# Filler writes spread over sixteen pairs, dummies of TensorE moved, and the last loads split over two queues

## The chip, the core and the metric

The kernel runs on one core of a Trainium2 chip. The metric is the device time of one execution in microseconds (us). The kernel before took 531.76 us, the median of three runs (530.24, 531.76, 532.05). A core has five engines that run side by side, each with its own instruction queue and in order: TensorE (PE) for matrix products, VectorE (DVE), ScalarE (ACT), GpSimd (POOL) and SyncE (SP), which here only issues transfers. They wait for each other through semaphores.

## What is computed

The reference, cut to what matters. `x` is 16 sequences of 512 tokens with 128 features.

```python
def wkv_layer(x):                       # first layer, added to x twice: inside and outside
    xn = layernorm(x, g1, b1)
    r, w, k, v = sigmoid(xn @ Wr.T), -exp(xn @ Ww.T), xn @ Wk.T, xn @ Wv.T
    e = exp(w + k)                      # a scan over the 512 tokens of a sequence:
    # num = decay * num + e * v ; den = decay * den + e ; wkv = num / (den + 1e-8)
    x = x + (r * wkv) @ Wo.T
    xn = layernorm(x, g2, b2)
    return x + sigmoid(xn @ Wrec.T) * (square(relu(xn @ Wkey.T)) @ Wval.T)

def moe_layer(h):                       # second layer: 16 experts, one for each token
    score, expert = top1(h @ router_w.T)
    s = sigmoid(score)
    gate, up = split((h * s) @ gate_up[expert])
    routed = (up * silu(gate)) @ down[expert]
    shared = (silu(h @ shared_gate.T) * (h @ shared_up.T)) @ shared_down.T
    return shared + routed

x = x + wkv_layer(layernorm(x))
out = x + moe_layer(layernorm(x))
```

## The kernel before, in words

**Tile stage.** The 8192 tokens are 16 tiles of 512, one sequence each. `one_round(n)` is written once for each engine; in round n the engine does step 0 of tile n, step 1 of tile n-1 and so on, in an order written out by hand, 23 rounds in all. For a tile: `T1` transposes the normed input `xn1tok`, `Ww`, `Wk`, `Wv`, `Wr` are products on it, the scan follows on VectorE, `Wo` gives `a`, whose normed form `an` is transposed (`T2`) into `xn2T`; then `K0` to `K3` (products with `Wkey`), their squares, `VAL0` to `VAL3`, the norm `h`, its transpose `hT`, the router and most of the shared expert. At the end of a tile its 512 rows, scaled, go with an indirect DMA into `sorted_rows` in memory, at the place of their expert: each of the 16 experts has a region. A row has 257 words: 128 of input, the token's number, and 128 of what is already known of its result.

**Dummies.** `warm(count)` issues products of `ident` with itself into a bank that nobody reads. Each f32 product is two passes in the profile, so 8 dummies read as x16. `WARM_FIRST` stand at the start, `WARM_BEHIND` behind `T1` of tiles 0 and 1, `WARM_BEFORE` ahead of `T1` of tiles 1 and 2 (L652 to L662).

**Expert stage.** The sorted rows are worked on in 80 slots of 128 rows, two to a pair, 40 pairs (`NP`), 44 turns. `one_turn(m)` on TensorE transposes the inputs of pairs m and m+1 where m is even, and does gate and up of pair m-2 and down of pair m-4. SP loads each pair (two loads of 128.5 KB) into a ring of 12 buffers (`RING`); from pair 12 on it waits until POOL's stores have freed the buffer of pair k-12. Those stores are indirect DMAs, one for each slot, to the token's row in `out` (L1271). Between the turns TensorE does `late_step`s: the shared expert for nine half tiles of the twelve `LATE` ones, whose result stays in SBUF (`sh_of`).

**Fillers.** A region is not filled to a whole slot, so 128 rows of `filler` are written behind the last row of each expert (`tail_i` has these places, `entries` reads such a table into registers), with a token number outside the output. Only slots from 48 on (`FULL_SLOTS`) can reach into them: SP waits for all of them before pair 24. All sixteen are issued before pair 12 (`FILL_PAIR`, L375 to L377).

**Tail.** When all stores have landed (`all_stored`), SP loads the twelve late half tiles of `out` back in six transfers (`load_late`), VectorE adds the shared expert's part, and SP and ScalarE store them, six each (`store_late`).

Of the kernel before, what the change touches and what calls it, by code (L numbers as in the profile page):

```python
# [28 lines left out]
P = 128  # L29
B, S, D = 16, 512, 128  # L30
F = 512
NE, EF, SF = 16, 128, 512
# [60 lines left out]
def program(nc, x, w_main, w_exp, vecs, out):  # L93
# [4 lines left out]
    with ExitStack() as ctx:  # L98
# [56 lines left out]
        late_to = xn1tok + xn1T + ew  # L155
# [68 lines left out]
        WARM_FIRST, WARM_BEFORE, WARM_BEHIND = 20, 8, 4  # L224
        FULL_SLOTS = NTOK // P - NE
        FILL_PAIR = 12
# [50 lines left out]
        def laps(i):  # L277

            return len(range(i, NP, RING))
# [28 lines left out]
        def tl_sem(u):  # L308

            return f"xr_in{u // 2}", 32 * laps(u // 2)  # L310
# [8 lines left out]
        def load_late(eng):  # L319
            halves_ = out.rearrange("(h p g) d -> p h (g d)", p=P, g=2)  # L320
            for u in range(0, N_LATE, 2):
                a0, a1 = first_row(u) // HALF, first_row(u + 1) // HALF
                eng.dma_start(shared[:, u * HALF:(u + 2) * HALF].rearrange("p (h c) -> p h c", h=2),  # L323
                              halves_[:, a0:a1 + 1:a1 - a0, :]).then_inc(s[tl_sem(u)[0]], 16)

        def store_late(eng, units):
            for u in units:
                eng.wait_ge(s["tl_add"], u + 1)
                eng.dma_start(out[first_row(u):first_row(u) + HALF, :].rearrange("(p g) d -> p (g d)", g=2), tl_of(u)).then_inc(
                    s["tl_out"], 16)  # L330
            eng.wait_ge(s["tl_out"], 16 * N_LATE)
# [10 lines left out]
        def _(sp):  # L342
# [30 lines left out]
            for k in range(NP):  # L373
                at_ = 2 * k % LOADED
                if k == FILL_PAIR:  # L375
                    for row in entries(SP_ENGINE, tail_i, 0, FILL_ROW - P, NE):
                        sp.dma_start(sorted_ap[bass.ds(row, P), :], filler[:, :]).then_inc(s["fill_out"], 16)  # L377
                if k == FULL_SLOTS // 2:
                    sp.wait_ge(s["fill_out"], 16 * (NE + 1))
                if at_ == 0 and k:  # L380
                    first_rows[:] = entries(SP_ENGINE, row_i, 2 * k, FILL_ROW, LOADED)
                if k >= RING:
                    sp.wait_ge(s[stored(k - RING)[0]], stored(k - RING)[1])
                for j in range(2):
                    sp.dma_start(xr[k % RING][:, j, :], sorted_ap[bass.ds(first_rows[at_ + j], P), :]).then_inc(  # L385
                        s[loaded(k)[0]], 16)
            all_stored(sp)
            load_late(sp)
# [4 lines left out]
        def _(pe):  # L393
# [76 lines left out]
            def one_round(n):  # L470
# [8 lines left out]
                for t in at(3):  # L479
                    wait(pe, "xn2T", t)  # L480
                    if t == 0:
                        pe.wait_ge(s["w_in1"], 16)
                    wait(pe, "hsg0", t - 2)
                    wait(pe, "sg0", t - 2)
# [24 lines left out]
                for t in at(3):  # L509
# [5 lines left out]
                    wait(pe, "xn2T", t)  # L515
                    wait(pe, "sg1", t - 2)
                    wait(pe, "hsg1", t - 2)
# [116 lines left out]
                for t in at(3):  # L634
                    wait(pe, "k20", t)
                    wait(pe, "hbase", t - 2)
                    wait(pe, "base", t - 2)
                    wait(pe, "cbase", t - 2)
# [4 lines left out]
                for t in at(2):  # L643
                    wait(pe, "an", t)
                    wait(pe, "a", t)
                    transposes(T2_B, an[t % 2], "T2")
# [5 lines left out]
                for t in at(0):  # L652
                    if t in (1, 2):
                        warm(WARM_BEFORE)
# [50 lines left out]
        def _(act_e):  # L705
# [147 lines left out]
            for m in range(TURNS):  # L853
                one_turn(m)
            store_late(act_e, range(1, N_LATE, 2))


        @block.vector
        def _(dve):
# [274 lines left out]
            for u in range(N_LATE):  # L1134
                if u % 2 == 0:
                    dve.wait_ge(s[tl_sem(u)[0]], tl_sem(u)[1] + 16)
# [178 lines left out]
```

## Time and profile before

| | |
|---|---|
| median of three runs | 531.76 us |
| profiled execution | 529.9 us |
| its span | 528.1 us |
| TensorE busy (matmul) | 491.6 us, 93% |
| VectorE busy | 399.9 us, 76% |
| POOL busy | 347.9 us, 66% |
| ScalarE busy | 323.3 us, 61% |
| DMA | 38.28 MB, mean 72 GB/s |

The span is the time from the first to the last instruction of the profiled execution. A row of the timeline has the start in us from the span's start, the length in us, the engine, the line, the operation, what it writes and reads, the count of like instructions merged in it, and in brackets how long the engine had stood idle before it and for whom. `SPq` and `ACTq` are transfers issued by SP and ScalarE, their length being that of the issuing. A row of the stretches has the stretch, its length, busy us and count for PE, PEld (weight loads), DVE, ACT and POOL, the clock granted to TensorE (1.00 is 2.4 GHz, 0.50 is 1.2 GHz), the mean busy share of the 16 DMA engines and the GB/s that they moved. Buffers are named by what they were first made for: in the tail `shared` holds the loaded half tiles, and the pairs' rows stand in `shared` and `rows`.

### The profile page before, as it was taken

How to read it: one execution, taken by the hardware profiler on the slowest of the kernel's cores; microseconds unless marked ns; L12 is line 12 of the kernel's file. 1: busy time of each engine (PE TensorE's matmuls, PEld its weight loads, DVE VectorE, ACT ScalarE, POOL GpSimd, SP SyncE). 2: the span in 40 equal slices, each digit the busy share in tenths (PEclk: the TensorE clock that was granted, in tenths of full speed). 3: DMA queues.
4: the chain of work that ended last, by engine and by line, in shares of the span. 5: the costliest groups of instructions: out<-in, count | busy, mean ns of one | idle time of the engine just before them, and what ended most of it. 6: DMA issues, size and time to landing. Idle time of an engine off the chain costs nothing. (4 is left out here: it accounts for less than half of the span.)

```text
span 528.1 us, 10490 instructions
## 1 busy us (share of the span) xinstructions
PE 491.6 (93%) x3100; PEld 406.4 (77%) x3100; DVE 399.9 (76%) x1100; ACT 323.3 (61%) x577; POOL 347.9 (66%) x542
## 2 busy tenths in 40 slices
PE   8687999999999999999999999999999969999970
PEld 7465678778787787877877778779988959999970
DVE  5958999997999979999799997974564525555413
ACT  5746977866778567785777857534225635665420
POOL 6544658885788857888578883674351747777770
PEclk9979999999999999999999999999999979999996
DMA  6003301010110101101011010011027974554107
GB/s 219 2 1 142 138 2 60 9 54 11 52 61 3 58 12 52 60 1 62 11 51 61 1 41 12 30 41 42 11 78 205 213 223 137 150 170 143 38 4 239
DMA packets 32296, 38.28 MB, mean 72 GB/s; under 512 B 4817, under 2 KB 28505, under 8 KB 31984
## 3 DMA queue, kind: packets, MB, share of 16 engines
q1 hardware_dynamic: 25776, 24.19, 15.9%
q0 software_dynamic: 5600, 12.63, 6.9%
q10 hardware_dynamic: 864, 0.79, 0.4%
q8 instruction: 26, 0.43, 0.4%
q14 instruction: 30, 0.25, 0.2%
HBM read 21.15 MB, written 17.41 MB: 73 GB/s over the span
## 5 line engine op out<-in xcount | busy, mean ns | idle before, releaser
L411 PE MATMUL bank<-hT,wm 128*128 128x256 f32 x512 | 121.6, 382 | 0.9 <-ACT er L752 0.7
L411 PEld LDWEIGHTS bank<-hT,wm 128*128 128x128 f32 x512 | 93.6, 190 | 18.1 <-issue 7.5
L1271 POOL DMA_INDIRECT out<-shared x55 | 54.1, 984 | 31.5 <-DVE shared L1123 16.3
L404 PE MATMUL bank<-wm,k 128*128 128x128 f32 x512 | 62.3, 275 | 2.8 <-ACT k L756 2.8
L404 PEld LDWEIGHTS bank<-wm,k 128*128 128x128 f32 x512 | 60.8, 192 | 4.4 <-ACT k L756 3.6
L885 DVE TENSOR_SCALAR an<-a,mvC,smC 128x128 f32<-128x128 f32 x64 | 43.2, 735 | 2.3 <-POOL smC L1171 2.3
L428 PEld LDWEIGHTS bank<-wm,actA 128*128 128x128 f32 x240 | 30.2, 192 | 6.7 <-issue 6.7
L1260 POOL TENSOR_SCALAR shared<-shared,smA 128x128 f32<-128x128 f32 x64 | 34.8, 552 | 0.2
L849 ACT ACTIVATE er<-bank 128x256 f32<-128x256 f32 x40 | 15.3, 384 | 27.2 <-PE bank L689 26.0
L428 PE MATMUL bank<-wm,actA 128*128 128x128 f32 x240 | 31.6, 275 | 0.0
L1271 POOL DMA_INDIRECT out<-rows x24 | 23.6, 983 | 12.0 <-issue 6.5
L1225 POOL DMA_INDIRECT sorted_rows<-rows,posi x16 | 21.4, 1335 | 9.3 <-DVE rows L982 3.3
L772 ACT ACTIVATE xn1tok<-shared,smA 128x128 f32<-128x128 f32 x62 | 25.4, 479 | 3.2 <-POOL smA L1207 3.2
L796 ACT ACTIVATE kr<-bank 128x512 f32<-128x512 f32 x16 | 9.6, 597 | 28.5 <-PE bank L486 28.5
L1255 POOL TENSOR_TENSOR q<-num,q 128x128 f32<-128x128 f32 x16 | 7.3, 454 | 28.3 <-DVE q L1056 28.3
L885 DVE TENSOR_SCALAR h<-rows,mvE,smE 128x128 f32<-128x128 f32 x64 | 23.1, 425 | 3.7 <-POOL smE L1171 3.5
L1123 DVE TENSOR_TENSOR shared<-bank,shared 128x256 f32<-128x256 f32 x28 | 11.9, 425 | 18.5 <-PE bank L695 18.5
L1244 POOL DMA_INDIRECT sorted_rows<-rows,posi x16 | 22.6, 1415 | 4.9 <-issue 4.9
L1215 POOL TENSOR_TENSOR smA<-smA,half 128x8 f32<-128x8 f32 x15 | 24.7, 1644 | 1.2
L1187 POOL TENSOR_SCALAR rows<-h,sc 128x128 f32<-128x128 f32 x64 | 22.6, 364 | 0.4
L1230 POOL TENSOR_TENSOR xa<-shared,a 128x512 f32<-128x512 f32 x16 | 21.1, 1317 | 0.5
L821 ACT ACT_TABLE_LOAD x16 | 20.5, 1283 | 0.3
(253 smaller groups left out, 1381.1 us busy)
## 6 DMA issues: line engine op xcount, KB each, us to landing
shared<-sorted_rows SPq DMA_DIRECT2D x56, 128.5 KB, 2.4
shared<-x SPq DMA_DIRECT2D x16, 256.0 KB
rows<-sorted_rows SPq DMA_DIRECT2D x24, 128.5 KB
wexp<-w_exp SPq DMA_DIRECT2D x2, 1536.0 KB, 8.4
sorted_rows<-filler SPq DMA_DIRECT2D x17, 128.5 KB
shared<-out SPq DMA_DIRECT2D x6, 256.0 KB, 5.6
sorted_rows<-rows,posi POOLq DMA_INDIRECT x64, 2.8
out<-shared POOLq DMA_INDIRECT x55, 2.8
```

The source lines that it names most:

```text
L404: ins = mm(grp(acc, g), grp(lhs, g), W(name, f), start=(f == 0 and g == 0), stop=(f == F // P - 1), skip_group_check=True)
L411: ins = mm(dst[:, j * HALF:(j + 1) * HALF], W(name, 2 * pair_ + j), src[:, half * HALF:(half + 1) * HALF], start=True, stop=True)
L428: ins = mm(grp(acc, 2 * half + g), lhs[:, at_:at_ + P], W("down", 2 * pair_ + j), start=(pair_ == 0 and j == 0 and g == 0), stop=(pair_ == ...
L772: ins = af(grp(xn1tok[t % 2], g), grp(xin[t % XR], g), ACT.Identity, bias=smA[t % 3][:, 5, g:g + 1], scale=smA[t % 3][:, 4, g:g + 1])
L885: ins = v.tensor_scalar(grp(dst, g), src(g), mv[:, g, 0:1], rs[:, g:g + 1], ALU.subtract, ALU.mult)
L1187: ins = g_.tensor_scalar(rows[t % 3][:, g, 0:D], grp(h[t % 2], g), sc[t % 2][:, g:g + 1], 1.0, ALU.mult, ALU.mult)
L1215: g_.tensor_tensor(sm[:, 3:5, :], sm[:, 1:3, :], half8[:, :, :], ALU.pow).then_inc(s["pA"], 1)
L1225: g_.indirect_dma_start(sorted_ap, bass.IndirectOffsetOnAxis(posi[t % 3][:, 1:2].bitcast(U32), 0), rows[t % 3][:, 1, :], None).then_inc(s[ ...
L1230: g_.tensor_tensor(xa[t % 3][:, :], xin[t % XR][:, :], a[t % 2][:, :], ALU.add).then_inc(s["xa"], 1)
L1244: g_.indirect_dma_start(sorted_ap, bass.IndirectOffsetOnAxis(posi[t % 3][:, 0:1].bitcast(U32), 0), rows[t % 3][:, 0, :], None).then_inc(s[ ...
L1260: ins = g_.tensor_scalar(grp(xn0[t % 4], g), grp(xin[t % XR], g), smA[t % 3][:, 0, g:g + 1], smA[t % 3][:, 3, g:g + 1], ALU.add, ALU.mult)
L1271: g_.indirect_dma_start(out, bass.IndirectOffsetOnAxis(xr[k % RING][:, j, D:D + 1].bitcast(U32), 0), xr[k % RING][:, j, D + 1:ROW], None, ...
```

## The change

It has three parts and some swapped lines.

- Fillers: `FILL_PAIRS` is pairs 4 to 19. The table of tails is read before pair 4, and one filler is issued ahead of each of these pairs. The wait before pair 24 stays.
- Dummies: `WARM_BEFORE` is a pair of numbers, 8 and 12. Eight stay ahead of `T1` of tile 1, those ahead of `T1` of tile 2 are gone, and twelve come ahead of `T2` of tile 0.
- Tail: a load for each of the twelve half tiles (128 KB), the even ones from SP, the odd ones from ScalarE, each with a semaphore of its own (`tl_sem`); VectorE waits for each.
- Three groups of waits on TensorE stand in another order, and `late_to` has one more entry.

```diff
-        late_to = xn1tok + xn1T + ew
+        late_to = xn1tok + xn1T + ew + kr[0:1]
...
-        WARM_FIRST, WARM_BEFORE, WARM_BEHIND = 20, 8, 4
+        WARM_FIRST, WARM_BEFORE, WARM_BEHIND = 20, (8, 12), 4
-        FILL_PAIR = 12
+        FILL_PAIRS = range(4, 4 + NE)
...
         def tl_sem(u):
-            return f"xr_in{u // 2}", 32 * laps(u // 2)
+            if u < 8:
+                return f"xr_in{u}", 32 * laps(u)
+            if u < 8 + XR:
+                return f"x_in{u - 8}", 16 * (NT // XR) + (32 * laps(u) if u < RING else 0)
+            return f"w_in{u - 8 - XR}", 16
...
-        def load_late(eng):
-            halves_ = out.rearrange("(h p g) d -> p h (g d)", p=P, g=2)
-            for u in range(0, N_LATE, 2):
-                a0, a1 = first_row(u) // HALF, first_row(u + 1) // HALF
-                eng.dma_start(shared[:, u * HALF:(u + 2) * HALF].rearrange("p (h c) -> p h c", h=2),
-                              halves_[:, a0:a1 + 1:a1 - a0, :]).then_inc(s[tl_sem(u)[0]], 16)
+        def place_of(u):
+            return out[first_row(u):first_row(u) + HALF, :].rearrange("(p g) d -> p (g d)", g=2)
+
+        def load_late(eng, units):
+            for u in units:
+                eng.dma_start(tl_of(u), place_of(u)).then_inc(s[tl_sem(u)[0]], 16)
...
             for k in range(NP):
                 at_ = 2 * k % LOADED
-                if k == FILL_PAIR:
-                    for row in entries(SP_ENGINE, tail_i, 0, FILL_ROW - P, NE):
-                        sp.dma_start(sorted_ap[bass.ds(row, P), :], filler[:, :]).then_inc(s["fill_out"], 16)
+                if k == FILL_PAIRS[0]:
+                    tails = entries(SP_ENGINE, tail_i, 0, FILL_ROW - P, NE)
+                if k in FILL_PAIRS:
+                    sp.dma_start(sorted_ap[bass.ds(tails[k - FILL_PAIRS[0]], P), :], filler[:, :]).then_inc(s["fill_out"], 16)
                 if k == FULL_SLOTS // 2:
                     sp.wait_ge(s["fill_out"], 16 * (NE + 1))
...
-            load_late(sp)
+            load_late(sp, range(0, N_LATE, 2))
             store_late(sp, range(0, N_LATE, 2))
...
+                    wait(pe, "sg0", t - 2)
                     wait(pe, "hsg0", t - 2)
-                    wait(pe, "sg0", t - 2)
...
                 for t in at(2):
+                    if t == 0:
+                        warm(WARM_BEFORE[1])
                     wait(pe, "an", t)
                     wait(pe, "a", t)
                     transposes(T2_B, an[t % 2], "T2")
...
                 for t in at(0):
-                    if t in (1, 2):
-                        warm(WARM_BEFORE)
+                    if t == 1:
+                        warm(WARM_BEFORE[0])
...
             for m in range(TURNS):
                 one_turn(m)
+            all_stored(act_e)
+            load_late(act_e, range(1, N_LATE, 2))
             store_late(act_e, range(1, N_LATE, 2))
...
             for u in range(N_LATE):
-                if u % 2 == 0:
-                    dve.wait_ge(s[tl_sem(u)[0]], tl_sem(u)[1] + 16)
+                dve.wait_ge(s[tl_sem(u)[0]], tl_sem(u)[1] + 16)
```

TensorE's queue around `T2` of tile 0, before: the last two products of tile 1, the transposes of `an`, eight dummies, the transposes of `xn1tok` of tile 2, and `K0` of tile 0.

```order
L582 MATMUL bank<-xn1T,wm 128x512 [waits ev,xn1T]
L592 MATMUL bank<-xn1T,wm 128x512 [waits er1,xn1T]
L398 MATMUL bank<-ident,an 128x128 [waits a,an]
L398 MATMUL bank<-ident,an 128x128 x3
L435 MATMUL bank<-ident 128x128 x8
L398 MATMUL bank<-ident,xn1tok 128x128 [waits xn1T,xn1tok]
L398 MATMUL bank<-ident,xn1tok 128x128 x3
L486 MATMUL bank<-xn2T,wm 128x512 [waits ew,w_in1,xn2T]
```

The same place now (lines are four further down):

```order
L586 MATMUL bank<-xn1T,wm 128x512 [waits ev,xn1T]
L596 MATMUL bank<-xn1T,wm 128x512 [waits er1,xn1T]
L439 MATMUL bank<-ident 128x128 x12
L402 MATMUL bank<-ident,an 128x128 [waits a,an]
L402 MATMUL bank<-ident,an 128x128 x3
L402 MATMUL bank<-ident,xn1tok 128x128 [waits xn1T,xn1tok]
L402 MATMUL bank<-ident,xn1tok 128x128 x3
L490 MATMUL bank<-xn2T,wm 128x512 [waits ew,w_in1,xn2T]
```

Twelve dummies stand ahead of the wait for `an`, and none between the transposes and `K0`.

SP's queue from the last load of pair 3 to the first of pair 5, before (`ISA` is the address arithmetic of a load):

```order
L385 DMA shared<-sorted_rows 128x257
L385 ISA
L385 DMA shared<-sorted_rows 128x257
L385 ISA
L385 DMA shared<-sorted_rows 128x257
L385 ISA
L385 DMA shared<-sorted_rows 128x257
```

and now:

```order
L389 DMA shared<-sorted_rows 128x257
L273 TENSOR_LOAD tail_i
L381 ISA
L381 DMA sorted_rows<-filler 128x257
L389 ISA
L389 DMA shared<-sorted_rows 128x257
L389 ISA
L389 DMA shared<-sorted_rows 128x257
L381 ISA
L381 DMA sorted_rows<-filler 128x257
L389 ISA
L389 DMA shared<-sorted_rows 128x257
```

The table's read and one filler have come ahead of pair 4, and a filler ahead of pair 5; the pattern goes on to pair 19, and the row of sixteen ahead of pair 12 is gone.

ScalarE's queue at its end, before:

```order
L728 ACTIVATE ew<-bank 128x256 [waits lD] x2
L329 DMA out<-shared 128x256 [waits tl_add] x6
```

and now:

```order
L734 ACTIVATE ew<-bank 128x256 [waits lD] x2
L328 DMA shared<-out 128x256 [waits scat2,xout11,scat1,xout0,scat0,xout1,xout7,xout2,xout6,xout3,xout5,xout4]
L328 DMA shared<-out 128x256 x5
L333 DMA out<-shared 128x256 [waits tl_add] x6
```

Its six loads have come behind the same wait for all stores that SP has.

## Rows read from the trace of the kernel before

**Rows 1.** Stretches, tile stage: busy us (count) per engine, clock, DMA share, GB/s.
```profile
60.00:390.00 330.00, 327.44 (x2001) 262.47 (x2000) 293.56 (x831) 222.04 (x369) 234.93 (x387) 1.00 0.10 34
```

**Rows 2.** Timeline, POOL's stores in the expert stage: start, length, engine, line.
```profile
412.80 0.98 POOL L1271 DMA_INDIRECT out<-shared  x1 [0.90 <-DVE shared L1123]
...
432.84 0.98 POOL L1271 DMA_INDIRECT out<-rows  x1 [4.89 <-DVE rows L1123]
...
512.79 0.98 POOL L1271 DMA_INDIRECT out<-shared  x1 [0.30 <-issue]
```

**Rows 3.** Timeline, the tail, SP's loads and VectorE's last additions.
```profile
515.03 3.14 SPq L323 DMA_DIRECT2D shared<-out  x6
...
523.87 0.76 DVE L1139 TENSOR_TENSOR shared<-shared,ew 128x256 f32<-128x256 f32 x2 [0.17 <-DMA shared<-out]
```

**Rows 4.** Timeline of TensorE in the first 48 us.
```profile
22.73 1.02 PE L592 MATMUL bank<-xn1T,wm 128*128 128x512 f32 x2
27.79 1.11 PE L398 MATMUL bank<-ident,an 128*128 128x128 f32 x4 [4.04 <-DVE an L885]
28.70 3.62 PE L435 MATMUL bank<-ident 128*128 128x128 f32 x16
...
32.93 1.02 PE L486 MATMUL bank<-xn2T,wm 128*128 128x512 f32 x2
...
47.45 0.66 PE L398 MATMUL bank<-ident,an 128*128 128x128 f32 x4 [0.72 <-DVE an L885]
```

**Rows 5.** Stretches behind TensorE's wait for `an` and of a later wait.
```profile
27.70:32.90 5.20, 5.11 (x24) 5.11 (x25) 5.17 (x8) 0.78 (x1) 2.38 (x6) 0.50 0.00 0
...
41.90:44.60 2.70, 0.01 (x1) 0.00 (x0) 2.33 (x11) 2.69 (x5) 1.08 (x2) 1.00 0.00 0
```

**Rows 6.** Timeline of ScalarE, `xn2T` of tile 0 and its next instruction.
```profile
28.95 0.78 ACT L788 ACTIVATE xn2T<-bank,vec 128x512 f32<-128x512 f32 x1 [2.26 <-PE bank L398]
33.99 0.60 ACT L796 ACTIVATE kr<-bank 128x512 f32<-128x512 f32 x1 [4.27 <-PE bank L486]
```

**Rows 7.** Timeline of VectorE, `an` of tile 0 and its longest wait behind it.
```profile
26.63 1.11 DVE L885 TENSOR_SCALAR an<-a,mvC,smC 128x128 f32<-128x128 f32 x4 [0.83 <-POOL smC L1171]
...
40.74 0.69 DVE L971 TENSOR_TENSOR ew<-bank,ew 128x512 f32<-128x512 f32 x1 [6.73 <-ACT ew L824]
```

**Rows 8.** Timeline of SP, loads and fillers up to pair 12 and behind.
```profile
394.58 8.56 SPq L385 DMA_DIRECT2D shared<-sorted_rows  x16
...
409.24 0.33 SPq L385 DMA_DIRECT2D rows<-sorted_rows  x1
...
410.91 8.11 SPq L377 DMA_DIRECT2D sorted_rows<-filler  x16
419.20 12.39 SPq L385 DMA_DIRECT2D shared<-sorted_rows  x16
```

**Rows 9.** Line L385: the two loads issued 399.7 to 400.4, six issued 418 to 423.
```profile
DMA to landing us min/median/max: 2.4/2.6/2.9
...
DMA to landing us min/median/max: 6.5/7.0/7.5
```

**Rows 10.** Timeline of TensorE, transposes of pairs 4 and 5, and of 12.
```profile
403.52 0.60 PE L681 MATMUL bank<-ident,shared 128*128 128x128 f32 x4
...
427.40 0.66 PE L681 MATMUL bank<-ident,shared 128*128 128x128 f32 x2 [4.67 <-DMA shared<-sorted_rows]
```

**Rows 11.** Stretches in the tail.
```profile
518.50:521.00 2.50, 0.00 (x0) 0.00 (x0) 0.94 (x4) 0.00 (x0) 0.00 (x0) 0.50 0.83 251
521.00:523.00 2.00, 0.00 (x0) 0.00 (x0) 1.41 (x5) 0.00 (x0) 0.00 (x0) 0.50 1.06 367
```

**Rows 12.** Waits of TensorE: us in total, times, longest.
```profile
PE bank L404 <- ACT k L756: 2.8, 1, 2.8
```

**Rows 13.** Stretches of the expert stage with fillers in flight.
```profile
415.00:420.00 5.00, 5.00 (x40) 4.74 (x39) 2.73 (x6) 3.01 (x7) 3.78 (x5) 1.00 1.10 225
420.00:425.00 5.00, 2.74 (x25) 2.54 (x23) 1.56 (x5) 2.80 (x7) 3.78 (x5) 1.00 1.05 145
```

More of the change, by code:

```diff
@@ L328, in store_late @@
                 eng.wait_ge(s["tl_add"], u + 1)
-                eng.dma_start(out[first_row(u):first_row(u) + HALF, :].rearrange("(p g) d -> p (g d)", g=2), tl_of(u)).then_inc(
-                    s["tl_out"], 16)
+                eng.dma_start(place_of(u), tl_of(u)).then_inc(s["tl_out"], 16)
             eng.wait_ge(s["tl_out"], 16 * N_LATE)
@@ L515, in one_round @@
                     wait(pe, "xn2T", t)
+                    wait(pe, "hsg1", t - 2)
                     wait(pe, "sg1", t - 2)
-                    wait(pe, "hsg1", t - 2)
                     wait(pe, "er1", t + 1, 1)
@@ L635, in one_round @@
                     wait(pe, "k20", t)
+                    wait(pe, "cbase", t - 2)
+                    wait(pe, "base", t - 2)
                     wait(pe, "hbase", t - 2)
-                    wait(pe, "base", t - 2)
-                    wait(pe, "cbase", t - 2)
                     wait(pe, "rv", t - 1)
```

## The prediction

> **What bounds the kernel now.** I read the stretches first. In the tile stage TensorE is busy 327.4 of 330 us and the DMA share is 0.10 [rows 1]: TensorE sets the pace, so what comes late once at its start shifts all behind it. The timeline of TensorE shows such a place near 28 us. In the expert stage (397 to 513 us) POOL sets the end: it issues 79 stores one behind the other, the fifth at 412.80, the last at 512.79; from 432.84 on it is 62 steps in 79.95 us, 1.29 each, and the one long hole is 4.89 us before 432.84 [rows 2]. The tail begins when the last store has landed: SP issues six loads from 515.03, VectorE makes twelve additions, the last pair from 523.87 on, each waiting on a load, and twelve stores go out [rows 3]. No matmul is in it.
>
> The profiled run took 529.9 us (span 528.1 and 1.8 around it). The sum is made against it and then carried to the median of the runs, 531.8, which lies 1.9 above it.
>
> **Part 1, dummies.** TensorE ends at 23.75, stands 4.04 us for `an` of tile 0, and starts its transposes at 27.79. Four of them take 1.11 us, then 16 dummy passes 3.62, then the transposes of tile 2, and only at 32.93 comes `K0` of tile 0 [rows 4]. From 27.7 to 32.9 the granted clock is 0.50, 1.2 of 2.4 GHz [rows 5]. `K0` needs `xn2T`, which ScalarE has ready at 28.95 + 0.78 = 29.73; ScalarE then sits 4.27 us until `K0` comes [rows 6]. So dummies and low clock stand in the path.
> New: twelve dummies go ahead of `an`. A pass at half clock is 3.62 / 16 = 0.226, at full clock half of it; 24 passes take 2.7, from 23.7 to 26.4, before `an` is there at 26.63 + 1.11 = 27.74 [rows 7]. They cost nothing. If the clock holds, four transposes take 0.66, as at 47.45 [rows 4]; ScalarE follows 0.05 behind: 27.79 + 0.66 + 0.05 + 0.78 + 0.08 = 29.36. Tile 2's transposes fit in between. `K0` comes 3.6 us earlier. What would be late next? VectorE's next step sits 6.73 us waiting for ScalarE [rows 7], and ScalarE's row is the one that waits for `K0`; all follow. Gain 3.6. If the clock falls as before, the 5.2 us at 0.50 [rows 5] are met by products instead of dummies and half of them is lost: gain 1.0. These are the two ends. The dummies before tile 1 stay.
>
> **Part 2, fillers.** Before, SP issues the 24 loads of 12 pairs from 394.58 (16 in 8.56 us), the last at 409.24, reads the table of tails (1.67 to the next issue instead of 0.52, so 1.15) and issues 16 fillers from 410.91 in 8.1 us; pair 12 goes out at 419.20 [rows 8]. Its loads and those of the next two pairs take 6.5 to 7.5 us to land; pair 5's two, before any filler, took 2.4 to 2.9 [rows 9]. TensorE waits 4.67 us for pair 12 at 427.40 [rows 10], and POOL's hole comes from that.
> New: one filler ahead of each of the pairs 4 to 19. At pair 12 SP has issued nine fillers, not sixteen, and issues the pair at about 419.2 - 7 x 0.52 = 415.6. TensorE wants it at 422.7 (427.40 - 4.67), so 6 us of landing are nearly hidden; besides, POOL has pair 7 to store until 427.95. The hole closes to the usual 0.30: POOL gains 4.6. It then issues without a hole to the end; TensorE waits for loads into buffers that POOL frees, so its end moves with POOL's.
> The price: SP reads the table (1.15) and issues two fillers (1.04) before pair 5's second load, the twelfth: 400.3 becomes 402.5, and with 2.9 of landing 405.4. TensorE transposes pair 5 from 403.52 + 0.22 [rows 10]. The wait, 1.7 to 2.0, I take as 1.8; it moves POOL's first store, which hangs on the same turn, and POOL, having no slack, never gets it back. Lower bound 1.2 (landing 2.4), upper 6 (landing 7.5). Behind it each pair shifts SP by 0.52 more: pair 9's second load, the twentieth, near 406 now, goes out at 406 + 1.2 + 6 x 0.52 = 410.3 and lands near 413.5, while TensorE wants it at 413.9 + 1.8. No further wait, if the DMA keeps up. Net 4.6 - 1.8 = 2.8; bounds -2 and 3.4.
>
> **Part 3, tail.** Before, six loads of 256 KB; the additions wait on each, the last until 523.85 [rows 3]. New: twelve of 128 KB, six on SP and six on ScalarE, which has nothing left to do by then. Each queue issues six, so issuing takes the same 3 us. What the queues move matters more: 251 GB/s at 518.5 to 521, when only SP's has packets, 367 once both move stores [rows 11]. The first 5 us at 251 are 1.26 MB; at 360 they take 3.5. Gain 1.4. Lower end -0.5: twelve loads waited for in order, one queue's share late. Upper end 2.7: the 1.57 MB at 360 GB/s are through at 520.4, and 0.7 of the difference I leave for landing.
> Against this speaks the Trainium skill ("DMA: Bandwidth & Descriptors", section "Issuing engines are not separate DMA queues"): transfers of several engines interleave on the same 16 DMA engines, and a second queue saves only issue time; by that the tail would gain nothing. The two rates disagree with it, but no row has loads on two queues at once.
>
> **At nothing.** The swapped waits in `K0`, `K2` and `VAL0` keep their semaphores and counts; before L404 TensorE waits once, 2.8 us [rows 12], for another reason (the squares). Both ends 0.5. The entry `kr` added to `late_to` is a seventh that no unit uses. The six more waits on VectorE lie behind loads.
>
> **Sum:** 529.9 - 3.6 - 2.8 - 1.4 = 522.1; against the median 531.8 - 7.8 = 524.0.
>
> **Rivals.**
> *A, the clock falls all the same.* TensorE still stands 1.4 us from 26.4 to 27.8 and 0.5 before `K0`. For it: it fell behind 4.04 us of standing. Against: it stayed at 1.00 through 2.7 us without work at 41.9 to 44.6 [rows 5]. Head 1.0: 526.6.
> *B, the tail gains nothing*: the DMA engines, not the queue, hold the loads at 251 GB/s. For it: they are busy 0.83 there. Against: they reach 367 two microseconds later [rows 11]. 525.4. The rule named in part 3 would come out so.
> *C, the fillers' wait only moves.* The loads of pairs 5 to 13 each land late behind a filler; TensorE waits in turns 4, 6, 8 and 12, and POOL gets the same hole in pieces. For it: landings of 6.5 to 7.5 us behind fillers [rows 9]. Against: there sixteen stood in a row. Middle 0 to -1: 527.3. It decides from 4.6 us of waits on.
> *D, slower: the DMA becomes the bound.* A pair with filler and two stores moves 3 x 131.6 + 2 x 65.5 = 526 KB while POOL takes 2.58 us, which asks for 204 GB/s. Rows with fillers in flight show 225 GB/s at 415 to 420, but 145 at 420 to 425, with the DMA engines fully busy in both [rows 13]. At 145 for all sixteen pairs, a pair takes 3.6 us: 16 x 1.05 = 17 us more; 531.8 - 3.6 - 1.4 - 4.6 + 17 = 539. It decides below 204 GB/s. Against it: over both rows the mean is 185 with fillers twice as dense as they will be.
>
> **How the numbers follow.** Forecast 0.52; A 0.14; B 0.14; C 0.13; D 0.04; a wait I don't see 0.03. What a measurement of this kernel can tell from no change is 0.3%, 1.6 us. Forecast, A, B and most of C lie beyond it: faster 0.92. Same 0.04 (A with C), slower 0.04 (D, part of the unseen). The likeliest case alone spans 522.2 to 526.2 (the wait of part 2 at 1.2 to 3, the tail at 0.3 to 2.7). The range of 8 in 10 takes in A, B and C, and goes a microsecond lower for runs as quick as the profiled one: 521.3 to 528.2.
>
> **What would show it.** Part 1: `K0` of tile 0 near 29.4, clock 1.00 from 23 to 38. Part 2: no wait in turn 12, one of about 1.8 us in turn 4 near 400; POOL's stores without a hole over 1 us, the last at 512.79 - 3.6 - 2.8 = 506.4. Part 3: over 300 GB/s in the tail's first 5 us, the last load landed 7.4 us after the first issue instead of 8.8. I am wrong if waits for loads in turns 6 to 14 sum to over 3 us, if POOL has a hole over 2 us, or if `K0` starts after 31.

## The result and the profile after

| | before | after |
|---|---|---|
| median of the runs, us | 531.15 (530.24 to 532.05, 4 runs) | 524.56 (524.07 to 525.79, 4 runs) |
| ratio, 95% interval | | 0.9879 [0.9853, 0.9906] |
| profiled run, span, us | 529.9, 528.1 | 524.36, 522.6 |
| `K0` of tile 0 starts | 32.93 | 29.91 |
| SP's first load of the expert stage | 394.58 | 391.73 |
| POOL's last store | 512.79 | 507.75 |
| first load of the tail | 515.03 | 509.98 |

The medians are 6.6 us apart, the ratio says 6.4 us faster (5.0 to 7.8), and the forecast was a median of 524.0. The two spans differ by 5.5 us: 2.85 are there at SP's first load, 5.04 at POOL's last store, 5.05 at the tail's first load. The tail makes up the remaining 0.45 in this pair of profiles.

TensorE around `T2` of tile 0 in the changed kernel (timeline; columns as in [rows 2]), which answers to [rows 4]:

```profile
23.32 1.02 PE L596 MATMUL bank<-xn1T,wm 128*128 128x512 f32 x2
24.18 2.84 PE L439 MATMUL bank<-ident 128*128 128x128 f32 x24
28.38 0.66 PE L402 MATMUL bank<-ident,an 128*128 128x128 f32 x4 [1.36 <-DVE an L893]
28.88 0.60 PE L402 MATMUL bank<-ident,xn1tok 128*128 128x128 f32 x4
29.91 1.12 PE L490 MATMUL bank<-xn2T,wm 128*128 128x512 f32 x2 [0.43 <-ACT xn2T L794]
```

Its stretch that answers to the first of [rows 5] (columns as in [rows 1]):

```profile
27.70:32.90 5.20, 4.08 (x21) 2.65 (x22) 5.17 (x9) 2.35 (x4) 1.79 (x5) 1.00 0.00 0
```

All of the first 30 us shift by up to 1.2 us from profile to profile, so I measure from the row of the last products ahead of `T2`, L592 before and L596 here, and call the distance `K0`'s delay: 32.93 - 22.73 = 10.20 us before [rows 4], 29.91 - 23.32 = 6.59 now. That is 3.61 us less. The four transposes take 0.66 instead of 1.11, and the granted clock stays at 1.00, the 2.4 GHz level.

Timeline of TensorE at pairs 4 and 5, and of POOL's stores, which answer to [rows 10] and [rows 2]:

```profile
401.80 0.41 PE L687 MATMUL bank<-ident,shared 128*128 128x128 f32 x2 [0.95 <-DMA shared<-sorted_rows]
403.60 0.44 PE L687 MATMUL bank<-ident,shared 128*128 128x128 f32 x2 [1.40 <-DMA shared<-sorted_rows]
```

```profile
406.65 1.00 POOL L1278 DMA_INDIRECT out<-shared  x1 [17.00 <-DVE shared L1131]
...
412.42 0.98 POOL L1278 DMA_INDIRECT out<-shared  x1 [0.90 <-DVE shared L1131]
...
427.88 0.98 POOL L1278 DMA_INDIRECT out<-rows  x1 [0.30 <-issue]
...
507.75 0.98 POOL L1278 DMA_INDIRECT out<-shared  x1 [0.31 <-issue]
```

The fifth store keeps its wait of 0.90; behind it POOL never stands longer than 0.31, and the hole of 4.89 us is gone. In its place TensorE has two waits for the loads of pairs 4 and 5, 2.35 us together. Counted from SP's first load, POOL's first store comes at +14.92 instead of +12.45, the last at +116.02 instead of +118.21.

The tail in the timeline, answering to [rows 3]:

```profile
508.35 0.38 ACT L734 ACTIVATE ew<-bank 128x256 f32<-128x256 f32 x1 [2.30 <-PE bank L423]
509.98 2.91 SPq L328 DMA_DIRECT2D shared<-out  x6
509.99 2.81 ACTq L328 DMA_DIRECT2D shared<-out  x6
512.35 1.68 DVE L1146 TENSOR_TENSOR shared<-shared,xn1tok 128x256 f32<-128x256 f32 x4 [6.88 <-DMA shared<-out]
512.94 6.01 SPq L333 DMA_DIRECT2D out<-shared  x6
513.18 6.18 ACTq L333 DMA_DIRECT2D out<-shared  x6
516.00 1.47 DVE L1146 TENSOR_TENSOR shared<-shared,xn1T 128x256 f32<-128x256 f32 x4 [1.96 <-DMA shared<-out]
517.41 1.51 DVE L1146 TENSOR_TENSOR shared<-shared,ew 128x256 f32<-128x256 f32 x4
```

The two queues issue side by side, and the last eight additions run without a wait that the timeline lists. Read from 518.3 on, the last row is this one, the additions of half tiles 10 and 11:

```profile
518.16 0.76 DVE L1146 TENSOR_TENSOR shared<-shared,ew 128x256 f32<-128x256 f32 x2
```

Half tile 10 is SP's last load, and its addition starts 8.2 us behind the first issue; the semaphore of that load has its last update in the trace at 518.14. Before, the last load was waited for until 8.8 us behind it [rows 3]. The row of ScalarE's copy is one to keep in mind: its last copy of a late product ends 1.25 us before its loads go out.

### The profile page after: what moved, and what is told of

Same layout as the page of the kernel before. It is cut to its first block and busy times, and to the rows that moved or that the text cites. A ratio compares the mean times of both kernels' runs of the same rounds, so it can differ in the third digit from the quotient of the medians.

```text
span 522.6 us, 10519 instructions
## 1 busy us (share of the span) xinstructions
PE 489.6 (94%) x3108; PEld 403.6 (77%) x3108; DVE 400.6 (77%) x1100; ACT 323.3 (62%) x577; POOL 347.8 (67%) x542
## 3 DMA queue, kind: packets, MB, share of 16 engines
q0 software_dynamic: 5600, 12.63, 6.8%
## 5 line engine op out<-in xcount | busy, mean ns | idle before, releaser
L893 DVE TENSOR_SCALAR an<-a,mvC,smC 128x128 f32<-128x128 f32 x64 | 43.2, 735 | 2.3 <-POOL smC L1178 2.3
## 6 DMA issues: line engine op xcount, KB each, us to landing
shared<-sorted_rows SPq DMA_DIRECT2D x56, 128.5 KB, 2.9
rows<-sorted_rows SPq DMA_DIRECT2D x24, 128.5 KB
sorted_rows<-filler SPq DMA_DIRECT2D x17, 128.5 KB
```

What stands on the lines that cost most here:

```text
L893: ins = v.tensor_scalar(grp(dst, g), src(g), mv[:, g, 0:1], rs[:, g:g + 1], ALU.subtract, ALU.mult)
```

## The experiments

The kernels of this section ran on three chips. On the first the kernel before took 530.0 us, and four kernels ran there; the changed kernel itself was not among them, so that its 0.9879 is from another measurement. Three of the four are the parts, each put alone into the kernel before, where a ratio against it is the part's own worth.

**The dummies alone.**

```diff
-        WARM_FIRST, WARM_BEFORE, WARM_BEHIND = 20, 8, 4
+        WARM_FIRST, WARM_BEFORE, WARM_BEHIND = 20, (8, 12), 4
...
+                    if t == 0:
+                        warm(WARM_BEFORE[1])
...
-                    if t in (1, 2):
-                        warm(WARM_BEFORE)
+                    if t == 1:
+                        warm(WARM_BEFORE[0])
```

> The kernel before with the dummies moved as in the change, fillers and tail as before. In the changed kernel K0 of tile 0 came 3.6 us earlier, measured from the last product of tile 1 ahead of it. If that shift is carried through the tile stage, this run is 3.6 us faster than before (ratio 0.993) and SP's first load of the expert stage comes near 391 in place of 394.6. Rival: part of it is absorbed later (a wait on an x load or on the expert weights); then the first load comes later than 392 and the time is 1 to 3 us faster.

Measured: 527.13 us, ratio 0.9932 [0.9907, 0.9958], 3.6 us (2.2 to 4.9). Its profile has the same delay of `K0`, 6.59 us. In this one profile the clock fell at another place, behind TensorE's wait for `k` (timeline, then stretches):

```profile
41.97 3.78 PE L404 MATMUL bank<-wm,k 128*128 128x128 f32 x16 [2.77 <-ACT k L758]
```

```profile
27.70:32.90 5.20, 3.88 (x20) 2.45 (x21) 5.17 (x10) 2.14 (x4) 1.58 (x4) 1.00 0.00 0
41.30:48.20 6.90, 6.23 (x29) 6.23 (x30) 6.07 (x9) 3.56 (x8) 3.40 (x5) 0.51 0.45 156
```

Before and after the change the clock held through the same wait (1.00 in the second of [rows 5]). From L592's row to SP's first load it takes 370.6 us, where the changed kernel takes 368.4: 2.2 us more, of which the products at the low clock are the visible part. So the mechanism of Rival A is real, at a place that I had cited against it. That place is worth counting over all profiles. In the three with the dummies as before (before, fillers alone, tail alone) the clock held there; of the nine with the new head and no dummies in that wait it held in two (the changed kernel's first, and the one with the fillers from pair 6) and fell in seven, the first row of `VAL0` taking 3.16 to 3.78 us instead of 2.05.

**The fillers alone.**

```diff
-                if k == FILL_PAIR:
-                    for row in entries(SP_ENGINE, tail_i, 0, FILL_ROW - P, NE):
-                        sp.dma_start(sorted_ap[bass.ds(row, P), :], filler[:, :]).then_inc(s["fill_out"], 16)
+                if k == FILL_PAIRS[0]:
+                    tails = entries(SP_ENGINE, tail_i, 0, FILL_ROW - P, NE)
+                if k in FILL_PAIRS:
+                    sp.dma_start(sorted_ap[bass.ds(tails[k - FILL_PAIRS[0]], P), :], filler[:, :]).then_inc(s["fill_out"], 16)
```

> The kernel before with the fillers one with each pair from pair 4, dummies and tail as before. Theory: the hole of 4.9 us in POOL's stores closes, and waits of some 2.3 us for pairs 4 and 5 are paid, net 2.2 us from SP's first load to POOL's last store, so 2.2 us faster (ratio 0.996). Rival: the gain hung on TensorE's clock, which stays full now, and is worth more when alone; or the waits depend on the phase of the transfers and take all of it: then 0 or 4.

Measured: 527.54, 0.9949 [0.9932, 0.9965], 2.7 us (1.9 to 3.6). POOL's first store is at +14.89 from the first load, the last at +116.08, with no hole: within 0.1 us the two numbers of the changed kernel.

**The tail alone** (its loads, its semaphores, and the swapped waits; the diff shows the loads).

```diff
-            load_late(sp)
+            load_late(sp, range(0, N_LATE, 2))
...
+            all_stored(act_e)
+            load_late(act_e, range(1, N_LATE, 2))
```

> The kernel before with the tail's twelve loads on two queues alone. In the changed kernel the last load landed 1.8 us sooner after the first issue than before, but the end only 0.5 us sooner. Theory: loads and stores together are bound by the DMA engines, so 0.5 us faster (ratio 0.999), not to be told from none by the times; the profile shows the end 12.6 us behind the first load in place of 13.1. Rival: the changed kernel's profile was an unlucky one and the tail is worth the 1.4 us of the prediction.

Measured: 529.56, 0.9984 [0.9969, 0.9999], 0.8 us (0.1 to 1.6). Its profile is longer than that of before, 530.9, because POOL had more to wait at pair 12 there:

```profile
434.84 0.98 POOL L1275 DMA_INDIRECT out<-rows  x1 [5.75 <-DVE rows L1128]
```

Head alone, which has the same row of sixteen fillers, shows 2.85 at that place. The holes that the fillers left come to 3 to 7 us, by the profile. In the three profiles with the row of sixteen POOL's last store is at +116.58, +118.21 and +120.39 from SP's first load; in the three on the first chip with the fillers spread it is at +115.33, +116.02 and +116.08. The three parts add to 7.2 us, the whole brought 6.4 (5.0 to 7.8), so no gain or loss by their being together can be seen.

The expectation takes the last load of the changed kernel to have landed 1.8 us sooner than before; by the row at 518.16 it was 0.7. The ends of the tail, counted from its first load, also scatter: 13.10, 12.61 and 12.45 us in the three profiles with the old tail (before, fillers alone, dummies alone), 12.78, 12.65 and 12.36 in the three with the new one on this chip. The profiles alone do not tell the two tails apart; the runs do, barely. Whether their 0.8 us come from the smaller loads or from the second queue is open, as the kernel that separates them ran on another chip only.

**No dummies at all at that place**: the changed kernel without the twelve.

```diff
-        WARM_FIRST, WARM_BEFORE, WARM_BEHIND = 20, (8, 12), 4
+        WARM_FIRST, WARM_BEFORE, WARM_BEHIND = 20, (8, 0), 4
```

> The changed kernel without its twelve dummies ahead of the transposes of tile 0 (none there, none ahead of tile 2). It tells the removal of the eight from the adding of the twelve. Theory: TensorE stands 4 us again, the clock falls to 0.50 near 26, the transposes take 1.1 us, K0 starts about 0.5 us later than with the twelve, and the products behind run at half clock for some 3 to 4 us: 2 to 2.6 us slower than the changed kernel. Rival: ScalarE and not TensorE sets the pace there, and the half clock costs 0.5 us only.

Measured: 526.6, 0.9947 [0.9921, 0.9973], against 0.9879 [0.9853, 0.9906] of the whole, from the other measurement: the intervals of the two part. Timeline of TensorE:

```profile
28.03 0.66 PE L402 MATMUL bank<-ident,an 128*128 128x128 f32 x4 [4.04 <-DVE an L893]
28.52 0.88 PE L402 MATMUL bank<-ident,xn1tok 128*128 128x128 f32 x4
29.55 2.08 PE L490 MATMUL bank<-xn2T,wm 128*128 128x512 f32 x2
31.42 1.37 PE L494 MATMUL bank<-xn2T,wm 128*128 128x512 f32 x2
```

`K0`'s delay is still 6.59 us; its products then run at the 1.2 GHz level (2.08 for two instead of 1.12), and again from 42.4 to 45.8 (0.51). SP's first load comes 1.8 us later behind L596's row than in the changed kernel. In this profile, then, taking the eight away moved `K0` and the lack of the twelve cost what follows: 1.8 us, half of the 3.6, while the two ratios are 3.6 us apart. Two things keep this from being settled. The queue up to the transposes of `an` is that of the kernel before, and there they ran at the low clock (1.11 us) in three profiles of three, here at the full one (0.66), so this one profile does not show that `K0` comes as early whenever the twelve are missing. And the clock fell behind `K0` in two profiles that have the twelve, as shown below.

The other eight ran on a second and a third chip, where the kernel before took 554.75 and 554.11 us. Up to the expert stage they are near those of the first: SP's first load of it stands at 392.4 to 393.7 in the profiles of all eight. The expert stage is not. **The changed kernel once more, on the third chip**, with its text as it was:

> The changed kernel as it is, beside the others. On the first chip it was 0.9879 of before. The four kernels that share its parts were last timed on a second chip, on which the kernel before takes 554.8 us, and came out at 1.002 to 1.010 of it there. If this run meets a chip like the first, 0.988 again, POOL's stores without a hole. If it meets one like the second, 1.00 to 1.006: then the change is worth nothing where the expert stage is not set by POOL.

Measured: 559.44, ratio 1.0066 [1.0031, 1.0102], slower than before. Timeline, a piece of its expert stage:

```profile
446.77 3.15 PE L415 MATMUL bank<-hT,wm 128*128 128x256 f32 x7 [0.93 <-issue]
446.87 0.69 DVE L1128 COPY er<-bank 128x512 f32<-128x512 f32 x1 [6.44 <-remote]
446.96 0.38 ACT L855 ACTIVATE er<-bank 128x256 f32<-128x256 f32 x1 [6.16 <-remote]
...
448.68 0.98 POOL L1278 DMA_INDIRECT out<-shared  x1 [3.42 <-DVE shared L1131]
```

The stretches of the stall and behind it (columns as in [rows 1]):

```profile
442.00:446.70 4.70, 1.47 (x6) 1.03 (x5) 0.00 (x0) 0.00 (x0) 2.66 (x3) 0.92 0.54 157
446.80:452.00 5.20, 5.20 (x18) 4.44 (x18) 3.40 (x7) 2.79 (x7) 2.71 (x3) 0.50 0.39 108
```

In 4.7 us TensorE does six products, with pauses in which the profile shows nothing that it waits for ("issue"); VectorE and ScalarE stand 6 us. Behind the stall TensorE's clock is at 0.50. Holes of 1.8 to 3.4 us in POOL's stores recur every 7 to 14 us, and the stage from SP's first load to POOL's last store takes 142.2 us instead of the 116.0 of its first profile; from 393 to 536 TensorE's clock is 0.92 on the mean, in the first profile 1.00. The profile names no cause for the pauses, all eight kernels profiled on the second and third chip have such a stage (140 to 145 us), and I leave it open. Where it leads is the tail:

```profile
538.03 2.91 SPq L328 DMA_DIRECT2D shared<-out  x6
...
544.51 0.42 DVE L1146 TENSOR_TENSOR shared<-shared,xn1tok 128x256 f32<-128x256 f32 x1
...
547.47 0.38 ACT L734 ACTIVATE ew<-bank 128x256 f32<-128x256 f32 x1 [2.31 <-PE bank L423]
547.91 2.80 ACTq L328 DMA_DIRECT2D shared<-out  x6
550.01 1.09 DVE L1146 TENSOR_TENSOR shared<-shared,xn1tok 128x256 f32<-128x256 f32 x3 [5.08 <-DMA shared<-out]
```

TensorE's late half tiles, which were done before the tail began on the first chip, now run past POOL's last store. ScalarE copies them and, being in order, issues its six loads only behind its last copy, 9.88 us after SP's. VectorE adds half tile 0 and stands 5.08 us for half tile 1. The span ends 19.3 us behind the first load of the tail instead of 12.65. All six kernels with loads on ScalarE that ran on these two chips show this: the loads go out 5.0 to 10.9 us behind SP's.

**Twelve loads from SP alone**, on the same chip:

```diff
-            load_late(sp, range(0, N_LATE, 2))
+            load_late(sp, range(N_LATE))
...
-            all_stored(act_e)
-            load_late(act_e, range(1, N_LATE, 2))
```

> The changed kernel with the tail's twelve loads all issued by SP, one behind the other, as twelve of 128 KB. It tells the splitting from the second queue. Theory: issuing takes 12 x 0.5 = 6 us on SP instead of 3, the DMA engines starve, the last load lands near 8.5 us after the first issue instead of 7.0, SP's stores start only behind 6 us, and the end comes 13.5 us or more after the first issue (12.6 in the changed kernel, 13.1 before). Rival, by the rule that a second queue gives nothing: the end at 12.6 again.

Measured: 555.11, ratio 0.9999 [0.9972, 1.0026]. Timeline:

```profile
539.18 5.86 SPq L328 DMA_DIRECT2D shared<-out  x12
...
547.30 1.42 DVE L1144 TENSOR_TENSOR shared<-shared,xn1tok 128x256 f32<-128x256 f32 x4
...
550.26 0.38 ACT L734 ACTIVATE ew<-bank 128x256 f32<-128x256 f32 x1 [2.31 <-PE bank L423]
550.27 2.88 ACTq L333 DMA_DIRECT2D out<-shared  x6
```

No load waits for ScalarE, VectorE's additions begin at +8.1 from the first load and run through, and the end is at +15.97. ScalarE's six stores still wait for its last copy, and the span ends 4.9 us behind that copy (550.26); in the changed kernel, where loads come behind it too, it ends 9.8 us behind (547.47). The other five with ScalarE's loads end 9.6 to 9.9 us behind it too. That is 4.9 us for the six loads' place; the ratios say 3.7, their intervals apart, and the two kernels differ in nothing else. The end itself, counted from the tail's first load, depends as much on when the late products are done: over the six it is between 14.4 and 20.1 us, so the 15.97 of this kernel's one profile neither bears out nor refutes the 13.5 expected. What the split or the second queue is worth where TensorE is done early is not shown by it.

At 0.9999 this kernel shows nothing of the 6 us of the first measurement. The kernel before has no profile on these chips, so where the gains of parts 1 and 2 went there is not shown; POOL's stores without holes, on which part 2 rests, do not occur there.

**ScalarE's loads left out**, same chip.

```diff
-            all_stored(act_e)
-            load_late(act_e, range(1, N_LATE, 2))
...
-                dve.wait_ge(s[tl_sem(u)[0]], tl_sem(u)[1] + 16)
+                if u % 2 == 0:
+                    dve.wait_ge(s[tl_sem(u)[0]], tl_sem(u)[1] + 16)
```

> The changed kernel with only the six loads of SP in the tail: the odd half tiles are not read back before they are added to and stored, so half of the output rows of the tail are not what they should be. 0.79 MB less is moved, the twelve additions and twelve stores remain. Theory: the tail is bound by the bytes of loads and stores together, at 315 GB/s over the stretch, so its end comes 2.5 us earlier, near 10.1 us after the first issue. Rival: the chain load, addition, store and its landing sets the end, and it comes 1 us earlier at most.

Measured: 553.12, 0.9952 [0.992, 0.9985]. Timeline:

```profile
537.63 2.91 SPq L328 DMA_DIRECT2D shared<-out  x6
...
540.84 1.42 DVE L1145 TENSOR_TENSOR shared<-shared,xn1tok 128x256 f32<-128x256 f32 x4
```

The additions begin at +3.2, and the end comes at +11.05, again 4.9 us behind ScalarE's last copy (543.80). Against twelve loads from SP the end comes 4.9 us earlier, and the last copy does too (+6.2 against +11.1), so the profiles show a chain that ends in TensorE's late products, not in bytes. The runs are 2.0 us apart. This kernel was to price the bytes of the loads; on a chip where TensorE comes last it can't.

**Where the 2.4 us at the start of the expert stage come from.** Two kernels:

```diff
             first_rows = list(entries(SP_ENGINE, row_i, 0, FILL_ROW, LOADED))
+            tails = entries(SP_ENGINE, tail_i, 0, FILL_ROW - P, NE)
...
-                if k == FILL_PAIRS[0]:
-                    tails = entries(SP_ENGINE, tail_i, 0, FILL_ROW - P, NE)
```

> The changed kernel with the table of tails read by SP right behind the first table of rows, while it still waits for the last scatter, instead of ahead of pair 4; fillers as in the change. In the changed kernel POOL's first store comes 14.9 us after SP's first load, against 12.5 before. Theory: of these 2.4 us the table's read is 1.15, so 13.8 here, and 1.2 us faster than the changed kernel. Rival: the fillers' bytes alone set the landing of pairs 4 and 5 (4 us against 2.9), and the pause of the read had given them room; then 14.5 and 0.4 us.

and with the same edit, one more:

```diff
-        FILL_PAIRS = range(4, 4 + NE)
+        FILL_PAIRS = range(6, 6 + NE)
```

> As the kernel with the early table, but fillers ahead of pairs 6 to 21 instead of 4 to 19. Theory: TensorE has 3 us and more of slack from turn 6 on, so nothing is late before POOL's first store: 12.5 us from first load to first store, no hole, and 2.4 us faster than the changed kernel (near 522). Rival: the fillers of pairs 6 to 12 are as late for turns 6 and 8, POOL gets small holes, and the gain is under 1 us.

Both ran on the second chip. By the runs they are 1.006 [1.0031, 1.0088] and 1.0018 [0.9979, 1.0057]; the intervals overlap, and neither expected gain shows. The start of the stage lies mostly ahead of the stalls. Timelines, POOL's first store of the one and of the other, from SP's first load (393.29 and 392.51) on:

```profile
407.13 1.00 POOL L1277 DMA_INDIRECT out<-shared  x1 [16.48 <-DVE shared L1130]
```

```profile
405.06 1.00 POOL L1277 DMA_INDIRECT out<-shared  x1 [15.18 <-DVE shared L1130]
```

That is +13.84 with the table read early and +12.54 with the fillers from pair 6 too (+12.92 in the profile of the kernel below that has both). The changed kernel has +14.92 in its first profile and +14.13 on the third chip, and the other profiles with its start of the stage lie between 14.1 and 14.9, but for one at +17.29, which has a stall ahead of that store; the kernel before has +12.45, and +12.46 and +12.63 in the two other profiles with its fillers. So the price is 1.5 to 2.5 us; 0.3 to 1.1 of it is the table's read, 0.9 to 1.3 the fillers of pairs 4 and 5, and most of it can be had back. What it is worth in time I could not show.

**Dummies in the wait for `k`, and the two together.**

```diff
+                    if t == 0:
+                        warm(10)
                     wait(pe, "k20", t)
```

> The changed kernel with ten more dummies ahead of VAL0 of tile 0, where TensorE stands 2.77 us for the squares of ScalarE. In two of the profiles so far the clock fell right behind that wait (at 41.3 in the one with the dummies alone, at 42.4 in the one without the twelve), in the others not. Theory: it is a matter of chance from run to run; with the wait filled it never falls, no run loses the 1.3 to 2.2 us, so the median is 0.5 to 1.5 us lower and the runs lie closer together. Rival: the dummies run over the end of the wait and cost what they save: same.

> The changed kernel with the table of tails read early, fillers with pairs 6 to 21, and ten dummies ahead of VAL0 of tile 0. On the second chip the run with the first two of these had POOL's first store 12.5 us behind SP's first load, as before the change, against 14.9 in the changed kernel. Theory: that is 2.4 us less, and 0.5 to 1.5 from the clock that can't fall in the tile stage: 3 to 4 us under the changed kernel in the same call (ratio to before near 0.981). Rival: fillers in turns 6 to 12 delay POOL elsewhere and the clock was not in the median: same as the changed kernel within 1 us.

The first kernel has this edit alone, the second has it with the early table and the fillers from pair 6. Measured: the first 557.37, 1.006 [1.0022, 1.0098] (second chip), the second 557.5, 1.0031 [0.9999, 1.0063] (third), where the changed kernel has 1.0066 [1.0031, 1.0102]. No two of these can be told apart; the 3 to 4 us expected of the second did not come. In both profiles the clock holds at 1.00 from 41 to 48, while the profiles of the changed kernel and of twelve loads from SP, without these dummies, have it at 0.50 to 0.51 from 43.2 to 46.6. Timeline, TensorE:

```profile
42.10 2.05 PE L408 MATMUL bank<-wm,k 128*128 128x128 f32 x16 [0.54 <-ACT k L764]
```

The products take 2.05 us and not 3.78. Without these dummies the clock fell there in seven profiles of nine; two of two in which it held are an indication and no more.

**The eight put back** behind the twelve, on the second chip:

```diff
-                    if t == 1:
+                    if t in (1, 2):
                         warm(WARM_BEFORE[0])
```

> The changed kernel with the eight dummies ahead of T1 of tile 2 put back, twelve kept. Theory: at full clock eight dummies take 1.8 us, of which 1.0 would have been waited for xn2T: K0 of tile 0 comes 1.3 us later than in the changed kernel, and the run is 1.3 us slower. With the run without the twelve this splits the head's 3.6 us: 1.3 for taking the eight away at full clock, and 2.3 that the eight cost more at half clock together with the slower transposes.

Measured: 561.88, 1.0103 [1.0048, 1.0157], from four runs. Timeline:

```profile
28.41 1.95 PE L439 MATMUL bank<-ident 128*128 128x128 f32 x16
...
30.63 1.02 PE L490 MATMUL bank<-xn2T,wm 128*128 128x512 f32 x2
```

L596's row starts at 22.85, so `K0`'s delay is 7.78 us instead of 6.59: at the full clock the eight cost 1.2 us. In the kernel before, at the low clock and with its slower transposes, `K0` came 3.6 later than in the changed one. The ratio is worse than the changed kernel's on the third chip, but the intervals overlap.

## Why the prediction was right, step by step

**Part 1 was right in place and size.** Forecast 3.6; `K0` moved by 3.61 behind L596's row, and alone the part gave 3.6 (2.2 to 4.9). Twelve dummies ran before `an` at the full clock and cost nothing. Two things in the argument were less sure than it said. It told removal and insertion as one; in the one profile without the twelve `K0` came as early, and 1.8 us went later, at the low clock. And Rival A, to which I gave 0.14, happened in the third chip's profile of the same kernel (stretch; mean clock 0.61):

```profile
28.50:32.90 4.40, 3.97 (x9) 1.64 (x8) 4.37 (x7) 1.37 (x2) 2.30 (x6) 0.61 0.00 0
```

There the two waits are 1.37 and 0.43 us, in the changed kernel's first profile, where it held, 1.36 and 0.43. It also fell there in the profile with twelve loads from SP, and held in the other seven of the nine with these two waits. From L596's row to SP's first load that profile of the changed kernel takes 370.8 us, 2.4 more than its first, with the fall behind the wait for `k` included. The row at 41.9 that I put against A was a place where, with the new head, it falls more often than not. That the 3.6 came in the runs and the forecast was met is in part luck with the clock. One execution's trace can't tell a clock that holds from a clock that held once.

**Part 2 was right in its places, and in size as far as it can be told.** Forecast: hole 4.6 gone, price 1.8, net 2.8. In the two profiles compared 4.59 went, the price was 2.47, the net 2.2; the runs of this part alone say 2.7 (1.9 to 3.6). Both terms scatter: without the twelve dummies the first store is at +14.14, a price of 1.7, and the hole was 2.85 to 5.75 in profiles with the row of sixteen. In the profile of the changed kernel the price is above the forecast at the landing: I took 2.9 us for pair 5's second load, from a stretch with loads alone [rows 9]. Lines L385 before and L389 after, loads issued from 398 to 404, where now a filler stands between every two:

```profile
DMA to landing us min/median/max: 2.4/2.8/3.2
...
DMA to landing us min/median/max: 3.1/3.6/3.7
```

I had also counted one wait, at pair 5; the first of the two, 0.95 us, is at pair 4, whose loads the table's read and a filler held up. Rival C did not come: from pair 6 on POOL has no hole. Nor did D: the two stretches of [rows 13] now show this:

```profile
415.00:420.00 5.00, 5.00 (x40) 4.74 (x39) 2.79 (x6) 3.17 (x9) 3.93 (x4) 1.00 0.79 195
420.00:425.00 5.00, 5.00 (x47) 5.00 (x46) 2.95 (x7) 3.67 (x10) 3.93 (x4) 1.00 0.82 194
```

The DMA engines move what is asked, near the 204 GB/s that I had worked out, and have a fifth of their time left. The 145 of before was no limit: TensorE stood for the loads from 422.7 on, and with the fillers spread the same stretch has 194.

**Part 3 is the step that failed, by its mechanism.** I took 251 GB/s for the rate of SP's queue alone and 360 for two queues. "Over 300 GB/s in the tail's first 5 us" did not come: the mean is 204, as it was before (200). The stretch of the changed kernel that answers to the first of [rows 11] has two queues at work and the same rate:

```profile
512.50:515.00 2.50, 0.00 (x0) 0.00 (x0) 1.41 (x4) 0.00 (x0) 0.00 (x0) 0.50 0.81 249
```

In forty slices of 0.375 us from the first load on, the tail before:

```profile
GB/s 0 0 8 90 246 369 385 292 268 281 262 238 178 232 270 314 352 361 372 374 382 380 382 372 333 374 306 350 369 167 57 27 22 0 0 0 0 0 0 0
```

and after:

```profile
GB/s 0 0 38 79 284 385 374 339 251 123 150 262 317 325 350 352 331 372 380 380 377 374 385 366 374 377 355 344 246 87 25 11 0 0 0 0 0 0 0 0
```

SP's queue alone, as no store is out yet, reaches 385 GB/s in the seventh slice; two queues reach the same 385. Then both kernels fall into a dip, 178 and 123, and come out of it (145 to 246 in the other four profiles of the first chip). My stretch lay across the dip of before; and the forecast laid its 251 on the first 5 us, where the mean was 200. So the rate of the stretch was not that of one queue. Rival B was right in that, and its result nearly came; what it put in the queue's place, the DMA engines holding the loads at 251 GB/s, does not explain a dip that both kernels leave again at 350 and more: the part alone gave 0.8 us (0.1 to 1.6), where I had forecast 1.4 and B none. In the two profiles the 3.15 MB of loads and stores, the same in both, are through some 0.5 us sooner, which is less than the scatter of 0.65 between profiles of one tail. The last load landed 8.2 us behind the first issue, not 7.4 as forecast (8.8 before). Behind the dip both kernels move loads and stores at 300 to 385 GB/s in nearly every slice until the end, whether the loads came from one queue or two. The Trainium skill ("DMA: Bandwidth & Descriptors", section "Issuing engines are not separate DMA queues") says that a second queue saves only issue time; these rows agree with it. What makes the dip is not shown.

The forecast held all the same: 7.8 us forecast, 5.5 in the two profiles, 6.4 to 6.6 in the runs; part 1 was as forecast, part 2 was 0.1 to 0.6 and part 3 0.6 to 1.0 too large. "ScalarE has nothing left to do by then" held by 1.25 us in the changed kernel's first profile and failed on the third chip. I wrote it down without reading its margin. There the place of the six loads costs 3.7 us, the whole difference between 1.0066 and 0.9999.

Where the kernel before takes 530 us, nothing that was run beat the changed one. On the third twelve loads from SP did (0.9999 against 1.0066, [0.9972, 1.0026] and [1.0031, 1.0102]). With the table early and the fillers from pair 6 it was not run.

## What to carry to other kernels

Before a transfer is given to an engine that also computes, read how long before it that engine's last computation ends: its queue is in order, and a margin of 1.25 us was gone on another chip. A rate read from one stretch is the rate of a queue only if the finer slices in it are level. Dummies for the clock belong where TensorE waits anyway; ahead of a product that others wait for they cost time even at the full clock, 1.2 us for these sixteen passes.

## What the runs showed of the hardware that I had not expected

- The granted clock is not settled by the instructions alone. Behind a wait of 2.77 us it fell in seven profiles (0.51 from 41.3 to 48.2 in one) and held in five; behind 1.36 and 0.43 us it held in seven and fell in two (0.61 on the mean of 28.5 to 32.9 in one), and the changed kernel has a profile of either kind.
- The same kernel takes 530 us on one chip and 554 to 555 on two others. Of the kernels profiled on both kinds the tile stage ends within 2 us of the same time; the expert stage is 24 to 29 us longer there, with pauses of TensorE that no wait of the program explains and a mean clock of 0.89 to 0.95 (393 to 533) instead of 1.00. A verdict can turn with it: 0.9879 in the first measurement, 1.0066 on the third chip.
- Sixteen 128.5 KB stores in one row ahead of loads opened a hole of 2.85, 4.89 and 5.75 us in three profiles of the same order; spread one to a pair they opened none in the three on the same chip.
